# Layer 1 of a two-layer kernel: the router and attention stage, the experts and the final sum in one block, loops written out

## The reference

```
x1 = output of layer 0;  xn = layernorm(x1)
q, k, v = xn @ Wq.T + bq, xn @ Wk.T + bk, xn @ Wv.T + bv
attn = softmax(q @ k.T / sqrt(128), axis=1)       # over the queries
a = attn @ v / sqrt(128)
m = xn * norm_scale * rsqrt(mean(xn**2) + 1e-6)   # rms norm
scores = m @ w_router.T                           # 8 experts
top 2 experts per token, weights = softmax of their two scores
f = sum over the two: weight * (down_e( u * silu(gate) )), (u, gate) = up_e(m)
out = x1 + a + (f + xn)
```

## Time and profile before

| what | value |
|---|---|
| median of 3 runs | 660.29 us (657.98 to 662.27) |
| the profiled execution | 659.7 us, its span 657.9 us |
| busy in the span | PE 539.2 (82%), DVE 449.9 (68%), ACT 358.6 (55%), POOL 307.0 (47%) |
| layer 0 | 0 to 360 us |
| layer 1's batch stage, tables | 360 to 490 us |
| experts | 497 to 632 us |
| sum | 639 us to the end |

### The profile page before, as it was taken

One profiled execution on the slowest core, in us unless ns is written; L12 is line 12 of the kernel. 1 busy time (PEld: TensorE's weight loads), 2 busy tenths in 40 slices (PEclk: granted clock), 3 DMA queues, 4 the chain that ended last, 5 costly groups with the idle time before them and its releaser, 6 DMA issues. The chain is left out here.

```text
span 657.9 us, 18248 instructions
## 1 busy us (share of the span) xinstructions
PE 539.2 (82%) x5803; PEld 315.1 (48%) x5804; DVE 449.9 (68%) x1874; ACT 358.6 (55%) x1069; POOL 307.0 (47%) x350
## 2 busy tenths in 40 slices
PE   5399999898998989899995898888635999999920
PEld 4134444444444444444443576556332666666610
DVE  7597898887878879788912698888751454545416
ACT  4404777777776776776773565666402444444410
POOL 6653736355461635610000378888740555555520
PEclk9655999999999999999997699999876999999965
DMA  3836181644627155370102511211111222222209
GB/s 96 175 101 125 51 178 36 156 101 119 131 64 163 55 143 103 95 150 4 35 27 74 212 50 51 68 56 56 57 53 33 70 74 75 73 73 75 72 19 368
DMA packets 51142, 61.14 MB, mean 93 GB/s; under 512 B 9969, under 2 KB 41973, under 8 KB 49280
## 3 DMA queue, kind: packets, MB, share of 16 engines
q1 hardware_dynamic: 45568, 49.67, 30.5%
q0 software_dynamic: 4352, 8.47, 3.8%
q10 hardware_dynamic: 1152, 2.10, 0.8%
HBM read 32.01 MB, written 28.45 MB: 92 GB/s over the span
## 5 line engine op out<-in xcount | busy, mean ns | idle before, releaser
L639 DVE CUSTOM_DVE_ANT_0 A<-A,band 128x320 f32<-128x320 f32 (+2 forms) x512 | 214.0, 463 | 47.6 <-PE A L801 46.6
L502 ACT ACTIVATE Pb<-SB 128x320 f32<-128x320 f32 (+2 forms) x512 | 175.4, 402 | 86.5 <-PE SB L837 84.4
L801 PE MATMUL A<-Ks,Qs 48*64 48x320 bf16 (+2 forms) x1024 | 131.9, 310 | 10.6 <-DVE mneg L639 4.4
L828 PE MATMUL SB<-Qs,Ks 50*64 50x320 bf16 (+2 forms) x1024 | 126.7, 294 | 12.6 <-ACT Pb L502 10.8
L828 PEld LDWEIGHTS SB<-Qs,Ks 50*64 50x64 bf16 x1024 | 55.9, 106 | 102.8 <-ACT Pb L502 85.7
L1603 POOL DMA_INDIRECT results<-y,xt x72 | 70.7, 982 | 71.3 <-issue 37.0
L837 PE MATMUL SB<-ends,ident 64*64 64x64 bf16 (+1 forms) x1024 | 98.1, 206 | 0.0
L850 PE MATMUL PV<-Pb,Va 128*32 128x320 f32 (+2 forms) x1024 | 86.4, 410 | 0.4 <-ACT Pb L502 0.4
L1707 PE MATMUL UP<-w_up,xT 128*128 x144 | 80.1, 639 | 1.6 <-ACT xT L1616 1.2
L1649 DVE COPY hT<-HT 128x256 f32<-128x256 f32 x72 | 30.5, 424 | 63.2 <-PE HT L1678 63.2
L1165 POOL DMA_INDIRECT expert_rows<-pay,pos x64 | 62.9, 982 | 22.9 <-issue 17.5
(11 more groups left out here) (225 smaller groups left out, 937.5 us busy)
## 6 DMA issues: line engine op xcount, KB each, us to landing
Qs<-parts_dram SPq DMA_DIRECT2D x16, 384.0 KB, 5.9
Ks<-parts_dram SPq DMA_DIRECT2D x16, 384.0 KB, 9.4
xt<-expert_rows SPq DMA_DIRECT2D x72, 65.0 KB, 1.8
yb<-results SPq DMA_DIRECT2D x8, 512.0 KB, 6.7
parts_dram<-qp SPq DMA_DIRECT2D x16, 192.0 KB, 2.9
parts_dram<-kp SPq DMA_DIRECT2D x16, 192.0 KB, 2.8
l_xb<-x_dram SPq DMA_DIRECT2D x9, 256.0 KB, 2.7
xb<-in_x SPq DMA_DIRECT2D x8, 256.0 KB, 2.9
```

What stands on the lines that cost most here:

```text
L502: act.activation(Pb[:, group % 4, c, 0:w], SB[k % NB_BANKS][:, 0:w], ACT.Exp).then_inc(act_exp, 1)
L639: nc.vector.tensor_tensor_reduce(scores_of, scores_of, band[:, skip:skip + w], -1.0, 3e38, ALU.add, ALU.min, mneg[:, step % 2, col:col + 1 ...
L801: mm = nc.tensor.matmul(A[k % NA_BANKS][out:out + HP, 0:w], Qs[b % RING][rows, a, HP * sub:HP * sub + HP], Ks[b % RING][rows, a, lo:lo + w ...
L828: nc.tensor.matmul(out[r0:r0 + HP, 0:w], Ks[b % RING][rows, a, HP * sub:HP * sub + HP], Qs[b % RING][rows, a, lo:lo + w], start=True, stop ...
```

## The change

- `layer1` and `experts` share one block. `experts` no longer opens a block; it returns one function per engine, called at the end of that engine's part of layer 1. `combine` is gone; its loads, additions and stores are the end of the experts' functions. PSUM banks are shared between the stages.
- All hardware loops of layer 1 and the experts are written out, without the passed-counters. NTILES is 71.
- x1 has a buffer of 8 batches (`xall`), all loaded early. x2b is attention + xn; x1 is added to x2b by DVE after tiles 8 to 15 of the experts (`residual`). `base_of` is gone; xn has three buffers.
- ACT makes the arguments of the roots (`arg_0`, `arg_1`); POOL only takes the powers.
- Router weights stand beside Wv (`wvr`, 136 columns), so that one matmul per tile makes values and router scores. Ranks take 5 matmuls.
- In the last batch `route_b` comes before the maxima, and the tables before its x2b.
- SP waits for all scattered rows itself. PE runs 20 matmuls (`WARM_X`) after the tables.

The diff, cut to its core:

```diff
-NTILES = -(-(TOKENS * TOPK + NE * (P - 1)) // P // 8) * 8
+NTILES = (TOKENS * TOPK + NE * (P - 1)) // P
+WARM_X = 20
...
     def _(sp):
-        def body(g, p, last, prior):
-            if not last:
-                wait(pool_base, g + 1)
-                ...
-                sp.dma_start(xb[p][:], xv[(g + 2) % NB]).then_inc(dma_x, 16)
+        for g in range(2, NB):
+            if g > 2:
+                sp.wait_ge(dma_x, 16 * (g - 2))
+            sp.dma_start(xall[:, g], xv[g]).then_inc(dma_x, 16)
...
+        sp.wait_ge(dve_fin, FIN)
+        for rows in dma_rows:
+            sp.wait_ge(rows, 16 * TOPK * NT * NB // 2)
+        after["sp"](sp)
...
         def roots(g, pg):
-            wait(act_sq, NT * (g + 1))
-            pool.tensor_scalar(arg[:, 1, :], ssq[:], 1.0 / P, 1e-6, ALU.mult, ALU.add).then_inc(pool_me, 1)
-            wait(dve_ag, NT * (g + 2))
-            pool.tensor_scalar(arg[:, 0, :], mv[:, :, 1], 1e-5, None, ALU.add).then_inc(pool_ve, 1)
-            ...
+            pool.wait_ge(act_arg1, g + 1)
+            pool.wait_ge(act_arg0, min(g + 1, NB - 1))
             pool.tensor_tensor(inv[pg][:], arg[:], mhalves[:], ALU.pow).then_inc(pool_inv, 1)
-        def base_of(g, pg):
-            ...
-            pool.tensor_tensor(base[pg][:], xb[pg][:], xn[pg][:], ALU.add).then_inc(pool_base, 1)
...
+        for g in range(NB):
+            if g + 1 < NB:
+                roots(g + 1, (g + 1) % 2)
+            scatter(g, g % 2)
+        after["pool"](pool)
...
+        def arg_0(g):
+            act.wait_ge(dve_ag, NT * (g + 1))
+            act.wait_ge(pool_inv, g)
+            act.activation(arg[:, 0, :], mv[:, :, 1], ACT.Identity, bias=eps[:, 0:1]).then_inc(act_arg0, 1)
+        def arg_1(g):
+            act.wait_ge(act_sq, NT * (g + 1))
+            act.activation(arg[:, 1, :], ssq[:], ACT.Identity, bias=eps[:, 1:2], scale=1.0 / P).then_inc(act_arg1, 1)
...
+        for g in range(NB):                        # ACT
+            p, last = g % 2, g == NB - 1
+            if last:
+                gate_exp(g)
+            else:
                 evac_xnT(g + 1)
             ...                                    # 4 exponentials
             if not last:
                 evac_q(g + 1, 1 - p)
+                gate_exp(g)
+                if g + 2 < NB:
+                    arg_0(g + 2)
                 evac_k(g + 1, 1 - p)
+                if g + 2 < NB:
+                    squares(g + 2)
+                    arg_1(g + 2)
+                rows_of(g + 1, 1 - p, (g + 1) // 2)
             scale_up(g)
+        after["act"](act)
...
+        for g in range(NB):                        # DVE
+            p, o, last = g % 2, 1 - g % 2, g == NB - 1
             if last:
                 ranks(g, last)
                 rows_to_pad()
+                route_b(g, p)
             ...                                    # maxima, ranks, stat, weights
-            route_b(g, p)
-            if not last:
+            if last:
+                tables()
+            else:
+                route_b(g, p)
                 evac_v(g + 1, o)
-                norm_of(g + 2, p)
+                if g + 2 < NB:
+                    norm_of(g + 2)
                 route_a(g + 1, o)
             dve.wait_ge(pe_out, g + 1)
-            dve.wait_ge(pool_base, g + 1)
-            nc.vector.tensor_tensor(x2b[:, bass.ds(g * NT, NT), :], OU[:].rearrange("p (i d) -> p i d", i=NT),
-                                    base[p][:], ALU.add).then_inc(dve_out, 1)
+            nc.vector.tensor_tensor(x2b[:, g * NT:(g + 1) * NT, :], OU[:].rearrange("p (i d) -> p i d", i=NT),
+                                    xn[g % 3][:], ALU.add).then_inc(dve_out, 1)
+        after["dve"](dve)
...
         def turn(g):                               # PE
             pe.wait_ge(dve_xn, NT * (g + 1))
             pe.wait_ge(dve_v, g)
+            if not (isinstance(g, int) and g == 0):
+                pe.wait_ge(dve_ra, RA * (g - 1) + 1)
...
         def rank(g, p, last):
+            out = RT[:, 0:NT * NE]
+            nc.tensor.matmul(out, tri[:], M[p][:].rearrange("p i e -> p (i e)"), start=True, stop=True)
+            for j in range(NT - 1):
+                nc.tensor.matmul(out[:, (j + 1) * NE:], ones[:], M[p][:, j, :].unsqueeze(1)
+                                 .to_broadcast([P, NT - 1 - j, NE]), start=False, stop=True,
+                                 skip_group_check=True)
+            mm = nc.tensor.matmul(out, ones[:], S[p][:].unsqueeze(1).to_broadcast([P, NT, NE]), start=False, stop=True,
+                                  skip_group_check=True)
...
         def values(g):
+            if not (isinstance(g, int) and g == 0):
+                pe.wait_ge(dve_rb, RB * (g - 1) + 1)
             for i in range(NT):
-                mm = nc.tensor.matmul(XV[:, i * P:(i + 1) * P], xnT[:, i * P:(i + 1) * P], wv[:],
+                mm = nc.tensor.matmul(blocks[:, i // 2, i % 2, :], xnT[:, i * P:(i + 1) * P], wvr[:],
                                       start=True, stop=True)
-        def router(g):
-            ...
...
+        pe.wait_ge(dve_fin, FIN)
+        pe.wait_ge(act_up, NB)
+        ...
+        for i in range(WARM_X):
+            nc.tensor.matmul(XR[:, 512:512 + P], ident[:], ident[:], start=True, stop=True)
+        pe.wait_ge(dve_out, NB)
+        after["pe"](pe)
...
+    def sp_part(sp):                               # experts
+        ...
+        for t in range(NTILES):
+            if t >= R:
+                sp.wait_ge(dma_y[t % R], 16 * (t // R))
+            load(t)
+        yv = yk.rearrange("(p b i k) d -> b p (i k d)", p=P, b=NB, i=NT)
+        for r in range(R):
+            sp.wait_ge(dma_y[r], 16 * turns(r))
+        for b in range(NB):
+            sp.dma_start(yb[:, b].rearrange("p i k d -> p (i k d)"), yv[b]).then_inc(dma_yb[b], 16)
...
+        def residual(b):                           # experts, DVE
+            rows = x2b[:, b * NT:(b + 1) * NT, :]
+            nc.vector.tensor_tensor(rows, rows, xall[:, b], ALU.add).then_inc(dve_res, 1)
+        for t in range(NTILES):
+            if t >= 1:
+                turned(t - 1)
+            dve.wait_ge(act_silu, t + 1)
+            ...                                    # h
+            if FIRST_RES <= t < FIRST_RES + NB:
+                residual(t - FIRST_RES)
```

More of the change, by code:

```diff
@@ L972, in layer1_inputs @@
     buf["mhalf"] = sb("mhalf", [P, NT])
-    buf["xb"] = [sb(f"xb{i}", [P, NT, P]) for i in range(2)]
+    buf["xall"] = sb("xall", [P, NB, NT, P])
     buf["x1s"] = sb("x1s", [P, NT, P])
@@ L976, in layer1_inputs, with layer1 @@
     return buf
[L979 removed]
+def layer1(nc, ctx, x1, buf, xs, x2b, tab, w_up, w_dn, w_up_in, w_dn_in, banks, after):
     def sb(name, shape, dt=F32):
@@ L1174, in _ @@
         pool.iota(nine_i[:], [[1, NE + 1]], base=0, channel_multiplier=0).then_inc(pool_const, 1)
-        wait(pool_const, NCP)
+        pool.wait_ge(pool_const, NCP)
         roots(0, 0)
-        base_of(0, 0)
-        def body(g, p, last, prior):
-            if not last:
-                roots(g + 1, 1 - p)
-                base_of(g + 1, 1 - p)
-            scatter(g, p)
-        batches(pool, body)
-        for rows in dma_rows:
-            wait(rows, 16 * TOPK * NT * NB // 2)
+        for g in range(NB):
[3 more added lines that the diff above has]
+        after["pool"](pool)
     @block.scalar
@@ L1565, in lag @@
-    def lag(t0, t, n):
-        return not isinstance(t0, int) or t0 + t >= n
-    def more(t0, r):
-        return not isinstance(t0, int) or t0 + r + 1 < NTILES
-    block = ctx.enter_context(nc.Block())
-    @block.sync
-    def _(sp):
-        def wait(sem, value):
-            sp.wait_ge(sem, value)
-            if not isinstance(value, int):
-                sp.sem_inc(sp_passed)
-        def load(t, r):
-            row = sp.value_load(tab[0:1, 0, bass.ds(t, 1)], min_val=0, max_val=NE * CAP)
-            sp.dma_start(xt[r][:], xs[bass.ds(row, P), :]).then_inc(dma_t[r], 16)
-        for r in range(R):
-            load(r, r)
-        with sp.Fori(1, NTILES // R) as i:
-            for r in range(R):
-                wait(dma_y[r], 16 * i)
-                load(R * i + r, r)
@@ L1664, in _ @@
-    @block.tensor
-    def _(pe):
-        def turn(t, r, before):
-            pe.wait_ge(dma_t[r], 16 * before)
-            nc.tensor.transpose(XT[r % 2][:, 0:P], xt[r][:, 0:P], ident[:]).then_inc(pe_xT, 1)
-        def expert_of(t):
-            return pe.value_load(tab[0:1, 1, bass.ds(t, 1)], min_val=0, max_val=NE - 1)
-        def turn_h(t, r, some):
+        evac_xT(0)
+        for t in range(NTILES):
+            if t + 1 < NTILES:
+                evac_xT(t + 1)
+            act.wait_ge(pe_up, t + 1)
+            if t >= 2:
+                act.wait_ge(dve_h, t - 1)
+            act.activation(sg[t % 2][:], UP[t % 2][:, HID:2 * HID], ACT.Silu).then_inc(act_silu, 1)
+            if t >= 2:
+                evac_y(t - 2)
@@ new lines, in expert_of @@
```

(18 more changed lines are left out.)

438 lines of the change are left out of this document (170 added, 268 removed).

## The result

The changed kernel takes 626.97 us, median of 4 runs (624.67 to 629.32); the kernel before took 659.87 in 4 runs beside it (657.98 to 662.27). Ratio 0.9499, 95% interval 0.947 to 0.9527. The prediction said 626, range 620 to 638. The profiled execution took 624.67 us, its span 622.9; it is the fastest of the four. Ratios are made from executions within 1.5% of a kernel's fastest, which only in run 12 leaves some out, two of four.

A forecast was written before the change was run, and what follows sets the result against it. POOL was taken to set layer 1's batch period and PE to bound the experts. Terms -1.2, -11.7, -3.2, -6.2, -6.1 and -5.8 sum to -34.2 us, against the median 626.1; predicted 626, range 620 to 638.

The forecast's parts named there:

- (a): Start of layer 1: first scatter comes earlier as DVE's wait before scores goes and S's sum shrinks, -1.2 us.
- (b): Layer 1's batch period: POOL loses arguments and base addition, 13.85 to 11.90 us, six periods -11.7.
- (c): Last batch: its addresses come before its maxima, so POOL's 3.54 us idle falls to 0.30, -3.2.
- (d): Join of layer 1 and experts: SP waits for rows in the same block, landing to load 6.5 becomes 0.3, -6.2 us.
- (e): Experts: one tile fewer -1.7, cold start -2.1, loop turns -2.3, residual additions hidden at 0; together -6.1 us.
- (f): The final sum: result landing to first load falls from 6.0 us to 0.2, -5.8.
- Rival 1: Layer 1's batches: DVE sets the period at 12.44 us, +3.2, 629.3 in all; chance 0.14.
- Rival 2: Layer 1's batches: hand-overs round DVE, ACT and PE keep the period at 13 to 13.85, 633 to 638 us; chance 0.12.
- The lock of the shared port: Layer 1's batches: DVE normalizations lock GpSimd out, POOL's time grows 1.11 us a batch, sum 632, by the skill's rule.
- Rival 4: Joins: the gap belongs to the DMA, not the block; (d) and (f) give nothing, +12, 638 us; chance 0.05.
- Rivals 3 and 5: Experts: 3, loop turns stay and residual additions delay PE, 628 to 634 (0.07); 5, instructions run out, 669 (0.03).

The follow-up runs named there:

- run 12: Changed kernel with the base addition back on POOL and the residual without it, on a chip with pauses: 660.34 us, ratio 0.9462.
- run 1: The changed kernel again, unaltered, as control: 628.53 us, ratio 0.9518.
- runs 1 to 4: On one chip: changed kernel again, with 36 warm matmuls, with none, with experts in their own block and POOL waiting: 628.53, 626.89, 626.49, 631.25 us.
- run 6: Changed kernel with the base addition back on POOL and no x1 additions in the experts, on a chip with pauses: 658.0 us, ratio 0.9514.
- run 9: Changed kernel with the base addition back on POOL and the residual without it, on a chip with pauses: 661.73 us, ratio 0.951.
- run 4: Changed kernel with the experts in a block of their own again and POOL waiting for the scattered rows: 631.25 us, ratio 0.9567.
- run 7: Changed kernel with the last batch's addresses after its maxima again, on a chip with pauses: 657.63 us in one execution.
- Runs 8 and 10: Changed kernel with POOL's power replaced by a subtraction, norms wrong, on chips with pauses: 659.84 and 664.98 us, one execution each.
- run 5: Changed kernel with the experts in a block of their own and SP waiting for the rows, on a chip with pauses: 664.4 us in one execution.

## Why the prediction held, step by step

From the milestones of the two profiled executions, us:

| step | forecast | measured | from |
|---|---|---|---|
| layer 0 | 0 | -2.3 | x1 stored 359.72, then 357.39 |
| (a) start | -1.2 | -1.6 | x1 stored to first scatter 23.43, 21.80 |
| (b) six periods | -11.7 | -11.95 | mean of the six 13.89, 11.90 |
| (c) last batch first | -3.2 | -3.0 | batch 6's first scatter to the last scatter 22.38, 19.35 |
| (d) join | -6.2 | -6.0 | gap 9.05, 3.07 |
| (e) cold start | -2.1 | -0.45 | first tile to third up product 6.21, 5.76 |
| (e) tiles | -4.0 | -3.8 | third up product to last result 124.83, 121.07 |
| (f) sum | -5.8 | -6.3, then +0.4 in the tail | gap 8.54, 2.27 |

Sum of the measured: -35.0, as the spans' 657.9 - 622.9. Layer 0 isn't touched; the same layer 0 ends anywhere from 356.20 to 361.93 in the other traces, so its 2.3 is the execution's own. Without it the steps gave 32.7 of the 34.2 forecast, and the medians differ by 32.9. Run 1's trace, a second one of the same kernel, gives 30.7: (a) to (d) and (f) are -1.2, -12.05, -3.1, -5.8 and -6.3, but its first tile to its last result took 128.59 us, against 131.04 before and 126.83 in the first profile. So (e) was worth 2.4 to 4.2 of the 6.1 forecast, and that the number came within 1 us is in part luck.

**(b), the largest step, was right in kind and size.** POOL without arguments and base addition needs 11.90 by the earlier trace rows; the trace shows 11.86 and no idle, and runs 1 to 4 have means of 11.87 to 11.88. That POOL is the bound rests on these rows; the runs that were to test it fell on chips with pauses. Rival 1 (DVE at 12.44) fell: DVE is 0.34 under POOL, and the floor without POOL's power is 11.5 by estimate. The prediction's 11.37 for DVE was a little low: normalizations cost 1.28 beside a scatter, where 1.11 had been taken. Rival 2, the ring, had its place in the same 11.5. Written out, scores to x2b took 2.16 where the loop took 2.96. The Trainium skill's rule (VectorE: DVE Perf Modes, "The DRAIN you can't avoid"), by which a semaphore costs nothing extra, would have left the chain as it was. But loop, registers and pass-counters went together and no run parted them, so the rule isn't disproved, only no guide to what a loop's chain costs. The lock of the shared port, which had been weighed as 1.11 a batch against this change, showed 0.13 on the first scatter (1.09 for 0.96) and 0.17 on the normalizations. (The 632 given for it by that rule is 6 x 1.11 above 625.5; above the median it would be 632.8.) Runs 6, 9 and 12 show DVE held for the whole of POOL's instruction where POOL computes.

**(c), (d) and (f)** came out within 0.5 each. Run 4 shows (d) alone: the block brings back the gap, though in the kernel's time it showed 2.7 us. Rival 4 (the gap is the DMA's) is out, since the load follows the landing by some 0.6 us once SP waits for it in the same block. (f) has the same shape, but its block was not tried alone. For (c) there is the profile's missing idle; run 7 could not size it.

**The mis-sized term is the cold start of (e)**, -2.1 forecast, -0.45 measured. The price was right: run 6 makes the stretch in 4.16, which is 2.05 under the 6.21 of before. Its condition was not. The prediction had the 20 matmuls start at about 469, 8.5 us ahead of the first tile at 477.5, and last 5.4 us at full clock: by its own numbers they left 3.1 us open, unless the clock was low. They started 8.29 ahead of the first tile, at full clock, and lasted 4.63, which left 3.67 us idle. That this hole would keep the clock was taken without a row for it. In run 1 the same 20 gained nothing (6.47, against 6.21 before). With 36 the hole shrank to 0.82, and the clock was still lost once the first tiles, which wait for ACT's copies (0.67 and 0.46 us), kept PE busy 1.3 to 1.5 us of 2. Runs 8 and 10, with holes of 0.74 and 1.13 and much the same shares, did not lose it. What decides between these is open.

**Tiles and residual additions** were right in kind: 68 tiles at 1.699 with no loop turns, and tiles 8 to 15 are 1.69 apart like the rest. In runs 1 to 4 the third up product to the last result took 120.63 to 122.60, so the -3.8 of the table is -2.2 to -4.2. Rivals 3 and 5 did not show in the first profile; a few tiles take 0.2 to 0.5 longer, none in a row.

## What to carry to other kernels

Take the bound from the order of time of one period, engine by engine, and then take off exactly what leaves it; busy shares of both kernels look alike here though one period is 2 us shorter. An elementwise addition on POOL can hold a DVE operation of 0.17 us until it ends itself (1.45 in run 9); ask whose next wait that lengthens. An engine that sets the period on one chip may stand idle for 4 us a batch on another, and an experiment on it then shows nothing. Read the gap at each block's end against the landing of the last transfer: what lies beyond it goes away when the stages share a block and the reader of the data waits for it itself.

## What was not expected of the hardware

- The end of a block costs 5.6 us past the landing of POOL's last indirect DMA (run 4), while between the two layers, where POOL had been idle for 75 us, the same join took 0.93, and in run 5 the next block began 1.40 after PE's last matmul.
- On three of the four chips of the runs PE, DVE and ACT paused in the batch stage, while POOL's scatters went on, and both kernels took 5% longer; the ratio stayed at 0.955 (0.9495 to 0.9601) there against 0.952 and 0.950. In the experts' stage those chips are nearly as fast as the first: third to last up product 115.5 to 118.7 against 115.1 to 117.0.
- PE kept full clock over 3.67 and 4.33 us of idle and lost it within 2 us after work had begun again (first profile, run 1); in run 7 it lost it during an idle of 4.20.
